# Four banks for a batch's four pieces, and the low-part product as half rows behind them

## The chip, the cores and the metric

The kernel runs on one core of a Trainium2 chip. Its time is the device time of one execution in microseconds, lower is better. Five engines work side by side, each through a queue of its own in order: TensorE (PE, with its weight loads shown apart as PEld), VectorE (DVE), ScalarE (ACT), GpSimd (POOL) and SyncE (SP), which starts the transfers. They wait for each other through semaphores.

## The reference

```python
W = weights[condition]                              # (64, 128, 128)
h = einsum('bct,bcd->bdt', x, W)                    # x: (64, 128, 2048)
logits = einsum('th,eh->te', flat(h), router_weight) + router_bias   # 64 experts, rows of 2048
scores = softmax(logits);  topk_w, topk_idx = top_k(scores, 8)
w_sum = topk_w.sum(-1);    w_dense = scatter of topk_w           # (8192, 64)
out = x + flat(h) * w_sum + w_dense @ expert_bias
```

All data is float32. A row is one of 128 outputs d of one of 64 batches, with 2048 elements t.

## The kernel before

Every matmul that needs float32 accuracy is split: an operand's high part is a copy rounded by ScalarE to the format that TensorE takes in one pass (names in `_hi`), its low part the rest, formed on VectorE or GpSimd (`_lo`), and products of parts are added up in PSUM.

Two batches make a pair (r = 0, 1), and a batch's 2048 columns are four pieces of 512 (n). A pair takes eight slots v. A step i of the pipeline holds three pairs at once: `new` is pair i, whose x is transposed and routed; `mid` is pair i - 1, whose logits, top 8, exponentials and kept weights are worked out; `old` is pair i - 2, which is projected, finished and stored. 32 pairs give 34 steps; 28 steps are a hardware loop of seven turns. The order on each engine is the order written in `step`, nothing reorders it:

- TensorE, slot v: `transposes(i, v)` (four 128x128 into a bank xt_ps; v = 2, 3 are done by VectorE's `relay` instead), `project(i-2, v)` into a bank p_ps, and in some slots `route` (eight matmuls of 256 columns: x transposed times router), `turn_z`, `score`, `turn_kept`.
- ScalarE copies each transposed piece (`xt_high`) and VectorE forms the rest (`xt_low`), which sets the bank free. ScalarE also does `x_high`, `exponentials`, `norm`, `kept_high`.
- VectorE: `xt_low(i, v)`, the top 8 and what follows, `finish(i-2, v)`, which takes a piece out of p_ps, scales it by w_sum, adds x and writes it to out_sb, and `relay`, which writes a transposed piece into a bank of xt_ps from x_turn.
- GpSimd forms x_lo; SyncE loads a batch when the finish eight batches back is done, and stores half a batch once its finishes are done.

PSUM has eight banks: four xt_ps, two p_ps, zt_ps and scores_ps. `project` adds five products per piece: three of x and W, then kept_t_hi and kept_t_lo, each times expert_hl. kept_t (the kept weights over w_sum, transposed) stands twice, in rows 0 to 63 and 64 to 127, and expert_hl holds the experts' high part above and the low part below, so that one product covers both.

Of the kernel before, what the change touches and what calls it, by code (L numbers as in the profile page):

```python
# [40 lines left out]
P = 128  # L41
# [9 lines left out]
def adaln_router(nc, x, condition, weights, router_weight, router_bias, expert_bias, out):  # L51
# [15 lines left out]
    with ExitStack() as ctx:  # L67
# [14 lines left out]
        expert_hl = sb("expert_hl", [P, T], F32R)  # L82

# [32 lines left out]
        xt_ps = [bank(f"xt_ps{i}") for i in range(4)]  # L116
        p_ps = [bank(f"p_ps{i}") for i in range(2)]
# [70 lines left out]
        def steps(eng, step):  # L188
            for j in range(-UNROLL, 0):
                i = UNROLL + j  # L190
                step(0, j, True, i >= 1, i >= 2)
            with eng.Fori(0, LOOPS) as m:
                for j in range(UNROLL):
                    step(m, j, True, True, True)
            step(LOOPS, 0, False, True, True)
            step(LOOPS, 1, False, False, True)
# [15 lines left out]
        def _(sp):  # L212
# [65 lines left out]
            for r in range(2):  # L278
                load(0, 3, r)
                load_weights(0, 3, r)  # L280
                if r == 0:
                    load_turned(0, 3)
                store(0, 0, r)
            with sp.Fori(0, LOOPS) as m:
                for i in range(UNROLL, 2 * UNROLL):
                    for r in range(2):
                        load(m, i, r)
                        load_weights(m, i, r)
                        if r == 0:
                            load_turned(m, i)  # L290
                        store(m, i - 3, r)
# [14 lines left out]
        def _(pe):  # L306
            def transposes(m, o, v):
# [10 lines left out]
                wait(pe, xt_lo_ready, SLOTS * (4 * m + o) + v - 3)  # L318
                for q in range(BLOCKS):
# [5 lines left out]
                    last = pe.transpose(xt_ps[v % 4][:, q * P:(q + 1) * P], block_of_x, ident[:, :])  # L325
# [46 lines left out]

            def project(m, o, v):
# [5 lines left out]
                wait(pe, finished, PIECES * b + n - 1)  # L379
                acc = p_ps[n % 2][:, :]  # L380
# [7 lines left out]
                if v == 0:  # L388
                    pe.wait_ge(kept_t_ready, 4 * m + o + 1)
# [18 lines left out]
            def step(m, j, new, mid, old):  # L408
                i = UNROLL + j
                for v in range(SLOTS):  # L410
                    if new and i == 2 and v < 4:
                        if v == 0:
                            for ahead in range(4):
# [4 lines left out]
                    if mid and v == 7 and i != 1:  # L418
                        turn_kept(m, i - 1)
                    if old:  # L420
                        if i == 2 and v == 0:
                            pe.wait_ge(expert_ready, 1)
# [6 lines left out]
                    if mid and v == 0:  # L429
                        route(m, i - 1, PIECES - 1)  # L430
                    if new and v in ((2, 4, 6) if old else (3, 5, 7)):
# [8 lines left out]
        def _(act):  # L440
            def xt_high(m, o, v):
# [6 lines left out]
                else:  # L448
# [3 lines left out]
                         xt_ps[v % 4][:, :].rearrange("p (q c) -> p q c", c=P)).then_inc(xt_hi_ready, 1)  # L452
# [58 lines left out]
            def step(m, j, new, mid, old):  # L511
                i = UNROLL + j
                for v in range(SLOTS):
# [28 lines left out]
        def _(dve):  # L542
            def xt_low(m, o, v):
                r, n = v % 2, v // 2
                dve.wait_ge(xt_hi_ready, SLOTS * (4 * m + o) + v + 1)
                dve.tensor_tensor(xt_lo[:, n % 2, :, r, :], xt_ps[v % 4][:, :].rearrange("p (q c) -> p q c", c=P),  # L546
                                  xt_hi[:, n % 2, :, r, :].bitcast(F32), ALU.subtract).then_inc(xt_lo_ready, 1)

            def relay(m, o, v):
# [5 lines left out]
                wait(dve, xt_lo_ready, SLOTS * i + v - 3)  # L555
                dve.transpose(xt_ps[v % 4][:, :].rearrange("p (q g c) -> p q g c", g=GROUPS, c=32),  # L556
# [46 lines left out]
            def finish(m, o, v):  # L603
# [8 lines left out]
                dve.scalar_tensor_tensor(out_sb[:, r, cols], p_ps[n % 2][:, :], w_sum[:, o % 2, r:r + 1],  # L612
# [11 lines left out]
            def step(m, j, new, mid, old):  # L624
                i = UNROLL + j
                for v in range(SLOTS):

                    if mid and v == 4:
# [89 lines left out]
```

## Time and profile before

| what | value |
|---|---|
| device time, median of three runs | 559.57 us (558.46 to 559.75) |
| profiled execution, own time | 558.69 us |
| its span | 556.9 us |
| granted TensorE clock, mean | 0.993 |
| busy: PE, DVE, ACT, POOL | 541.0, 471.2, 368.5, 354.4 us |
| DMA | 155.96 MB, 280 GB/s |

The span is the part of the execution that the profile's rows cover. Busy times of PE come from matmuls whose ends are modelled and which overlap, so the distance from one start to the next tells more than a duration.

### The profile page before, as it was taken

How to read it: one execution, taken by the hardware profiler on the slowest of the kernel's cores; microseconds unless marked ns; L12 is line 12 of the kernel's file. 1: busy time of each engine (PE TensorE's matmuls, PEld its weight loads, DVE VectorE, ACT ScalarE, POOL GpSimd, SP SyncE). 2: the span in 40 equal slices, each digit the busy share in tenths (PEclk: the TensorE clock that was granted, in tenths of full speed). 3: DMA queues.
4: the chain of work that ended last, by engine and by line, in shares of the span. 5: the costliest groups of instructions: out<-in, count | busy, mean ns of one | idle time of the engine just before them, and what ended most of it. 6: DMA issues, size and time to landing. Idle time of an engine off the chain costs nothing.

```text
span 556.9 us, 12892 instructions
## 1 busy us (share of the span) xinstructions
PE 541.0 (97%) x3360; PEld 477.0 (86%) x3360; DVE 471.2 (85%) x1055; ACT 368.5 (66%) x836; POOL 354.4 (64%) x326
## 2 busy tenths in 40 slices
PE   5879999999999999999999999999999999999997
PEld 5768888888888888888888888888888888888875
DVE  2488898988889988889988889898888998888975
ACT  3576666677666677666677666667666667766661
POOL 0176666766666776666776666676666677666676
PEclk9979999999999999999999999999999999999999
DMA  8986999888999888898888999888899888889245
GB/s 243 311 201 231 309 297 279 292 300 287 297 318 276 269 311 289 295 325 280 292 276 296 294 311 300 271 290 297 286 298 315 284 283 295 288 294 326 119 166 212
DMA packets 70850, 155.96 MB, mean 280 GB/s; under 512 B 6322, under 2 KB 45234, under 8 KB 62770
## 3 DMA queue, kind: packets, MB, share of 16 engines
q1 hardware_dynamic: 70834, 155.77, 85.6%
q8 instruction: 7, 0.11, 0.1%
q14 instruction: 9, 0.07, 0.0%
HBM read 88.64 MB, written 67.11 MB: 280 GB/s over the span
## 4 chain that ended last, share of the span: by engine, by line
PE 93%; DMA 3%; SPq 1%; ACT 1%; issue 1%; DVE 1%; ACTq 0%; DVEq 0%
PE zt_ps L337 21%; PE xt_ps L325 14%; PE p_ps L390 11%; PE p_ps L387 11%; PE p_ps L385 11%; PE p_ps L386 10%; PE p_ps L391 10%; PE scores_ps L360 2%; DMA out_sb<-L_ffn_expert_bias 2%; PE scores_ps L369 1%; PE scores_ps L351 1%; DMA cond_sb<-itok_B 1%; SPq L243 0%; SPq L244 0%; DVE xt_lo L546 0%
## 5 line engine op out<-in xcount | busy, mean ns | idle before, releaser
L681 POOL TENSOR_TENSOR x_lo<-x_sb,x_hi 128x512 fp32r<-128x512 f32 x256 | 327.0, 1308 | 176.2 <-ACT x_hi L459 176.2
L546 DVE TENSOR_TENSOR xt_lo<-xt_ps,xt_hi 128x512 fp32r<-128x512 f32 x256 | 175.7, 687 | 63.6 <-ACT xt_hi L451 60.8
L451 ACT CAST xt_hi<-xt_ps 128x512 fp32r<-128x512 f32 x256 | 148.2, 582 | 102.9 <-PE xt_ps L325 84.9
L612 DVE SCALAR_TENSOR_TENSOR out_sb<-p_ps,w_sum,x_sb 128x512 f32<-128x512 f32 x256 | 189.6, 740 | 6.2 <-PE p_ps L391 6.2
L459 ACT CAST x_hi<-x_sb 128x1024 fp32r<-128x1024 f32 x128 | 133.7, 1045 | 0.5 <-PE p_ps L391 0.5
L337 PE MATMUL zt_ps<-xt_hi,router_hl 128*128 128x256 f32 x512 | 129.6, 285 | 4.5 <-DVE xt_lo L546 4.5
L337 PE MATMUL zt_ps<-xt_lo,router_hl 128*128 128x256 f32 x512 | 129.2, 285 | 0.0
L325 PE MATMUL xt_ps<-ident,x_sb 128*128 128x128 f32 x784 | 119.2, 277 | 0.1
L385 PE MATMUL p_ps<-x_hi,w_hl 128*128 128x512 f32 x256 | 118.8, 464 | 0.0
L337 PEld LDWEIGHTS zt_ps<-xt_hi,router_hl 128*128 128x128 f32 x512 | 98.1, 192 | 11.0 <-DVE xt_lo L546 5.2
L337 PEld LDWEIGHTS zt_ps<-xt_lo,router_hl 128*128 128x128 f32 x512 | 98.4, 192 | 4.8
L325 PEld LDWEIGHTS xt_ps<-ident,x_sb 128*128 128x128 f32 x784 | 95.0, 145 | 8.5 <-DMA x_sb<-x 0.5
L390 PE MATMUL p_ps<-expert_hl,kept_t_hi 128*128 128x512 f32 x256 | 101.7, 397 | 0.0
L387 PE MATMUL p_ps<-x_hi,w_hl 128*128 128x512 f32 x256 | 101.2, 395 | 0.0
L386 PE MATMUL p_ps<-x_lo,w_hl 128*128 128x512 f32 x256 | 100.5, 393 | 0.0
L391 PE MATMUL p_ps<-expert_hl,kept_t_lo 128*128 128x512 f32 x256 | 100.2, 391 | 0.0
L556 DVE STREAM_TRANSPOSE xt_ps<-x_turn 128x512 f32<-128x512 f32 x60 | 67.2, 1120 | 0.0
L390 PEld LDWEIGHTS p_ps<-expert_hl,kept_t_hi 128*128 128x128 f32 x256 | 48.1, 188 | 11.6 <-DVE kept_t_lo L599 0.8
L391 PEld LDWEIGHTS p_ps<-expert_hl,kept_t_lo 128*128 128x128 f32 x256 | 48.3, 189 | 11.3
L387 PEld LDWEIGHTS p_ps<-x_hi,w_hl 128*128 128x128 f32 x256 | 48.2, 188 | 10.7
L478 ACT ACTIVATE e_all<-logits,neg_max 128x64 f32<-128x64 f32 x64 | 21.8, 340 | 44.1 <-DVE neg_max L579 44.1
L385 PEld LDWEIGHTS p_ps<-x_hi,w_hl 128*128 128x128 f32 x256 | 48.8, 191 | 1.9 <-issue 1.4
(38 smaller groups left out, 368.7 us busy)
## 6 DMA issues: line engine op xcount, KB each, us to landing
out<-out_sb SPq DMA_DIRECT2D x126, 512.0 KB, 4.2
x_sb<-x SPq DMA_DIRECT2D x62, 1024.0 KB, 6.8
x_turn<-x SPq DMA_DIRECT2D x120, 128.0 KB, 4.7
w_sb<-L_cond_weights SPq DMA_DIRECT2D x64, 64.0 KB, 5.3
x_sb<-x SPq DMA_DIRECT2D x4, 256.0 KB, 6.0
x_sb<-x SPq DMA_DIRECT2D x2, 512.0 KB, 8.0
out_sb<-L_ffn_expert_bias SPq DMA_DIRECT2D x2, 512.0 KB, 9.4
out<-out_sb SPq DMA_DIRECT2D x4, 256.0 KB, 2.5
```

Of the source, the lines that this page charges most:

```text
L325: last = pe.transpose(xt_ps[v % 4][:, q * P:(q + 1) * P], block_of_x, ident[:, :])
L337: last = pe.matmul(zt_ps[:, 0:2 * P], router_hl[:, t, :, :].rearrange("p a e -> p (a e)"), xt[:, n % 2, q, :, :].rearrange("p r c -> p (r ...
L385: pe.matmul(acc, w[:, 0, :], x_hi[:, r, cols], start=True, stop=False)
L386: pe.matmul(acc, w[:, 0, :], x_lo[:, r, cols], start=False, stop=False)
L387: pe.matmul(acc, w[:, 1, :], x_hi[:, r, cols], start=False, stop=False)
L390: pe.matmul(acc, kept_t_hi[:, o % 2, r, :], expert_hl[:, cols], start=False, stop=False)
L391: pe.matmul(acc, kept_t_lo[:, o % 2, r, :], expert_hl[:, cols], start=False, stop=True).then_inc(p_ready, 1)
L451: act.copy(xt_hi[:, n % 2, :, r, :], xt_ps[v % 4][:, :].rearrange("p (q c) -> p q c", c=P)).then_inc(xt_hi_ready, 1)
L459: act.copy(x_hi[:, r, cols], x_sb[:, (2 * o + r) % XRING, cols]).then_inc(x_hi_ready, 1)
L546: dve.tensor_tensor(xt_lo[:, n % 2, :, r, :], xt_ps[v % 4][:, :].rearrange("p (q c) -> p q c", c=P), xt_hi[:, n % 2, :, r, :].bitcast(F32) ...
L612: dve.scalar_tensor_tensor(out_sb[:, r, cols], p_ps[n % 2][:, :], w_sum[:, o % 2, r:r + 1], x_sb[:, (2 * o + r) % XRING, cols], ALU.mult, ...
L681: pool.tensor_tensor(x_lo[:, r, cols], x_sb[:, (2 * o + r) % XRING, cols], x_hi[:, r, cols].bitcast(F32), ALU.subtract).then_inc(x_lo_read ...
```

## The change

- **Banks.** xt_ps has two banks in place of four, p_ps four in place of two, one per piece. `transposes` and `relay` of slot v wait for the `xt_low` two slots back, no longer four. `project` of piece n waits for the finish of piece n of the batch before.
- **Products.** `project` leaves out kept_t_lo (but for the last batch). `add_kept_low` does it for all four pieces behind the batch's last projection: kept_t_lo times the experts' high part alone, in half of the rows, pieces 0 and 2 in rows 0 to 63, pieces 1 and 3 in rows 64 to 127. A new tile expert_hh holds the high part in both halves for that. Low part times low part is left out.
- **Finishes.** They come half a pair later: batch 0's four in slots 4 to 7 of its own step, batch 1's in slots 0 to 3 of the next step, each at the start of its slot.
- **Order.** Route 3 moves ahead of projection 0 and route 1 ahead of projection 4. SyncE's stores move by one batch.

```diff
+        expert_hh = sb("expert_hh", [P, T], F32R)
...
-        xt_ps = [bank(f"xt_ps{i}") for i in range(4)]
-        p_ps = [bank(f"p_ps{i}") for i in range(2)]
+        xt_ps = [bank(f"xt_ps{i}") for i in range(2)]
+        p_ps = [bank(f"p_ps{i}") for i in range(PIECES)]
...
                 for i in range(UNROLL, 2 * UNROLL):
-                    for r in range(2):
-                        load(m, i, r)
-                        load_weights(m, i, r)
-                        if r == 0:
-                            load_turned(m, i)
-                        store(m, i - 3, r)
+                    load(m, i, 0)
+                    load_weights(m, i, 0)
+                    load_turned(m, i)
+                    store(m, i - 4, 1)
+                    load(m, i, 1)
+                    load_weights(m, i, 1)
+                    store(m, i - 3, 0)
...
-                wait(pe, xt_lo_ready, SLOTS * (4 * m + o) + v - 3)
+                wait(pe, xt_lo_ready, SLOTS * (4 * m + o) + v - 1)
...
-                wait(pe, finished, PIECES * b + n - 1)
-                acc = p_ps[n % 2][:, :]
+                wait(pe, finished, PIECES * b + n - PIECES + 1)
+                acc = p_ps[n][:, :]
...
-                pe.matmul(acc, kept_t_lo[:, o % 2, r, :], expert_hl[:, cols],
-                          start=False, stop=True).then_inc(p_ready, 1)
+                if is_last(m, o, r):
+                    pe.matmul(acc, kept_t_lo[:, o % 2, r, :], expert_hl[:, cols],
+                              start=False, stop=True).then_inc(p_ready, 1)
+
+            def add_kept_low(m, o, r):
+                pe.wait_ge(kept_t_ready, 4 * m + o + 1)
+                for n in range(PIECES):
+                    rows = slice(n % 2 * E, (n % 2 + 1) * E)
+                    pe.matmul(p_ps[n][:, :], kept_t_lo[rows, o % 2, r, :],
+                              expert_hh[rows, n * PIECE:(n + 1) * PIECE],
+                              start=False, stop=True).then_inc(p_ready, 1)
...
+                    if mid and v == 0:
+                        route(m, i - 1, PIECES - 1)
+                    if new and old and v == 4:
+                        route(m, i, 1)
                     if old:
...
                         project(m, i - 2, v)
                     if mid and v == 3:
                         score(m, i - 1)
+                    if old and v % PIECES == PIECES - 1 and not is_last(m, i - 2, v // PIECES):
+                        add_kept_low(m, i - 2, v // PIECES)
...
-                        act.copy(expert_hl[:, :], expert_sb).then_inc(expert_hi_ready, 1)
+                        act.copy(expert_hh[:, :], expert_sb).then_inc(expert_hi_ready, 1)
+                    if i == 1 and v == 7:
+                        act.copy(expert_hl[0:E, :], expert_sb[0:E, :]).then_inc(expert_hi_ready, 1)
...
-                wait(dve, xt_lo_ready, SLOTS * i + v - 3)
-                dve.transpose(xt_ps[v % 4][:, :].rearrange("p (q g c) -> p q g c", g=GROUPS, c=32),
+                wait(dve, xt_lo_ready, SLOTS * i + v - 1)
+                dve.transpose(xt_ps[v % 2][:, :].rearrange("p (q g c) -> p q g c", g=GROUPS, c=32),
...
+                    if older and v < PIECES:
+                        finish(m, i - 3, PIECES + v)
+                    if old and v >= PIECES:
...
+                        finish(m, i - 2, v - PIECES)
                     if mid and v == 4:
                         dve.wait_ge(logits_ready, 4 * m + i)
                     if new:
...
-                        finish(m, i - 2, v)
```

The first place is TensorE's queue in the loop where batch 0 of a pair ends and batch 1 begins (slots 3 and 4). xt_ps and p_ps carry their bank numbers; ISA and REGISTER_ALU rows set up waits. Before:

```order
L390 MATMUL p_ps1<-expert_hl,kept_t_hi 128x512
L391 MATMUL p_ps1<-expert_hl,kept_t_lo 128x512
L357 ISA
L360 MATMUL scores_ps<-z_sb,w_sb 128x64 x2
L183 REGISTER_ALU
L325 MATMUL xt_ps0<-ident,x_sb 128x128 x4
L378 ISA
L183 REGISTER_ALU
L384 REGISTER_ALU
L385 MATMUL p_ps0<-x_hi,w_hl 128x512
```

Now:

```order
L396 MATMUL p_ps3<-expert_hl,kept_t_hi 128x512
L360 ISA
L363 MATMUL scores_ps<-z_sb,w_sb 128x64 x2
L407 MATMUL p_ps0<-expert_hh,kept_t_lo 128x512
L407 MATMUL p_ps1<-expert_hh,kept_t_lo 128x512
L407 MATMUL p_ps2<-expert_hh,kept_t_lo 128x512
L407 MATMUL p_ps3<-expert_hh,kept_t_lo 128x512
L184 REGISTER_ALU
L328 MATMUL xt_ps0<-ident,x_sb 128x128 x4
L336 REGISTER_ALU
L340 MATMUL zt_ps<-xt_hi,router_hl 128x256
```

The low-part products of all four pieces now stand together between the score and the next batch's transposes, and a route follows the transposes.

The second place is VectorE's queue at the start of a step (slots 0 and 1, and the start of 2 in the second listing). xt_lo rows are `xt_low`, STREAM_TRANSPOSE is `relay`, SCALAR_TENSOR_TENSOR is `finish`. Before:

```order
L546 TENSOR_TENSOR xt_lo<-xt_ps0,xt_hi 128x4x128
L183 REGISTER_ALU
L611 ISA
L612 SCALAR_TENSOR_TENSOR out_sb<-p_ps0,w_sum,x_sb 128x512
L183 REGISTER_ALU
L556 STREAM_TRANSPOSE xt_ps2<-x_turn 128x512
L545 REGISTER_ALU
L546 TENSOR_TENSOR xt_lo<-xt_ps1,xt_hi 128x4x128
L611 REGISTER_ALU
L612 SCALAR_TENSOR_TENSOR out_sb<-p_ps1,w_sum,x_sb 128x512
L556 STREAM_TRANSPOSE xt_ps3<-x_turn 128x512
```

Now:

```order
L636 SCALAR_TENSOR_TENSOR out_sb<-p_ps0,w_sum,x_sb 128x512
L569 ISA
L570 TENSOR_TENSOR xt_lo<-xt_ps0,xt_hi 128x4x128
L580 STREAM_TRANSPOSE xt_ps0<-x_turn 128x512
L635 REGISTER_ALU
L636 SCALAR_TENSOR_TENSOR out_sb<-p_ps1,w_sum,x_sb 128x512
L569 REGISTER_ALU
L570 TENSOR_TENSOR xt_lo<-xt_ps1,xt_hi 128x4x128
L580 STREAM_TRANSPOSE xt_ps1<-x_turn 128x512
L635 REGISTER_ALU
L636 SCALAR_TENSOR_TENSOR out_sb<-p_ps2,w_sum,x_sb 128x512
```

The finish of a slot now stands ahead of the slot's xt_lo and belongs to the batch before; the relay writes the same bank that the xt_lo ahead of it reads.

## Rows read from the trace of the kernel before

**Rows 1.** The chain that ended last, by engine.

```profile
PE 93%; DMA 3%; SPq 1%; ACT 1%; issue 1%; DVE 1%; ACTq 0%; DVEq 0%
```

**Rows 2.** The same chain in time: start us, us, what.

```profile
289.06 0.96 PE zt_ps L337 x8
...
305.59 0.96 PE zt_ps L337 x8
```

**Rows 3.** Stretch: engine busy us (instructions), granted clock, DMA share, GB/s.

```profile
289.06:305.59 16.53, 16.53 (x106) 14.66 (x106) 14.71 (x34) 11.38 (x27) 11.01 (x11) 1.00 0.90 292
```

**Rows 4.** Timeline of TensorE in a pair: start us, us, what.

```profile
291.01 0.55 PE L360 MATMUL scores_ps<-z_sb,w_sb 128*128 128x64 f32 x4
291.40 0.61 PE L325 MATMUL xt_ps<-ident,x_sb 128*128 128x128 f32 x4
291.76 0.47 PE L385 MATMUL p_ps<-x_hi,w_hl 128*128 128x512 f32 x1
292.08 0.39 PE L386 MATMUL p_ps<-x_lo,w_hl 128*128 128x512 f32 x1
...
292.77 0.39 PE L391 MATMUL p_ps<-expert_hl,kept_t_lo 128*128 128x512 f32 x1
293.00 0.28 PE L337 MATMUL zt_ps<-xt_hi,router_hl 128*128 128x256 f32 x1
...
293.96 0.60 PE L325 MATMUL xt_ps<-ident,x_sb 128*128 128x128 f32 x4
...
298.53 0.38 PE L369 MATMUL scores_ps<-ident,kept_twice 128*128 128x128 f32 x2
298.67 0.47 PE L385 MATMUL p_ps<-x_hi,w_hl 128*128 128x512 f32 x1
...
299.91 0.60 PE L325 MATMUL xt_ps<-ident,x_sb 128*128 128x128 f32 x4
```

**Rows 5.** One source line, router transposes: duration ns, first and last start.

```profile
L405 PE MATMUL p_ps<-ident,x_sb x16: 311/311/362, 4.8 to 7.8; 64*128 64x64 f32 x16
```

**Rows 6.** Timeline of TensorE behind the router transposes.

```profile
8.05 1.54 PE L325 MATMUL xt_ps<-ident,x_sb 128*128 128x128 f32 x6
```

**Rows 7.** Timeline of VectorE in a pair.

```profile
288.45 1.12 DVE L556 STREAM_TRANSPOSE xt_ps<-x_turn 128x512 f32<-128x512 f32 x1
289.46 0.68 DVE L546 TENSOR_TENSOR xt_lo<-xt_ps,xt_hi 128x512 fp32r<-128x512 f32 x1
...
295.74 0.69 DVE L546 TENSOR_TENSOR xt_lo<-xt_ps,xt_hi 128x512 fp32r<-128x512 f32 x1 [0.80 <-ACT xt_hi L451]
296.35 0.21 DVE L591 SCALAR_TENSOR_TENSOR e_kept<-e_all,e_rest 128x64 f32<-128x64 f32 x1
...
296.86 0.75 DVE L612 SCALAR_TENSOR_TENSOR out_sb<-p_ps,w_sum,x_sb 128x512 f32<-128x512 f32 x1
...
301.25 0.69 DVE L546 TENSOR_TENSOR xt_lo<-xt_ps,xt_hi 128x512 fp32r<-128x512 f32 x1
301.85 0.74 DVE L612 SCALAR_TENSOR_TENSOR out_sb<-p_ps,w_sum,x_sb 128x512 f32<-128x512 f32 x1
302.51 1.12 DVE L556 STREAM_TRANSPOSE xt_ps<-x_turn 128x512 f32<-128x512 f32 x1
```

**Rows 8.** Timeline of ScalarE in a pair.

```profile
295.15 0.56 ACT L451 CAST xt_hi<-xt_ps 128x512 fp32r<-128x512 f32 x1
...
300.62 0.59 ACT L451 CAST xt_hi<-xt_ps 128x512 fp32r<-128x512 f32 x1 [0.83 <-PE xt_ps L325]
```

**Rows 9.** Group by line: count, busy us, mean ns, idle ahead.

```profile
L520 ACT CAST expert_hl<-out_sb 128x2048 fp32r<-128x2048 f32 x1 | 1.9, 1909 | 2.1 <-DMA out_sb<-L_ffn_expert_bias 2.1
```

**Rows 10.** SyncE's waits: us in total, times, longest.

```profile
SPq L225 <- DVE out_sb L612: 248.5, 98, 8.2
```

**Rows 11.** Two early stretches, columns as in rows 3.

```profile
19.00:25.60 6.60, 5.23 (x41) 4.83 (x42) 3.29 (x6) 3.29 (x8) 0.87 (x2) 1.00 0.97 265
31.30:33.40 2.10, 2.08 (x9) 2.08 (x10) 1.80 (x7) 2.10 (x7) 1.83 (x2) 0.50 1.16 238
```

More of the change, by code:

```diff
@@ L324, in transposes @@
                             "c (k j) -> c j k", k=P)[:, q, :]
-                    last = pe.transpose(xt_ps[v % 4][:, q * P:(q + 1) * P], block_of_x, ident[:, :])
+                    last = pe.transpose(xt_ps[v % 2][:, q * P:(q + 1) * P], block_of_x, ident[:, :])
                 last.then_inc(xt_in_ps, 1)
@@ L371, in turn_kept, with is_last @@
                 last.then_inc(kept_t_in_ps, 1)
+            def is_last(m, o, r):
+                return not is_loop(m) and 8 * m + 2 * o + r == B - 1
             def project(m, o, v):
@@ L406, in _, with step @@
             last.then_inc(router_in_ps, 1)
-            def step(m, j, new, mid, old):
+            def step(m, j, new, mid, old, older):
                 i = UNROLL + j
                 for v in range(SLOTS):
-                    if new and i == 2 and v < 4:
+                    if new and i == 2 and v < 2:
                         if v == 0:
-                            for ahead in range(4):
+                            for ahead in range(2):
                                 transposes(m, i, ahead)
@@ L425, in step @@
                         score(m, i - 1)
+                    if old and v % PIECES == PIECES - 1 and not is_last(m, i - 2, v // PIECES):
+                        add_kept_low(m, i - 2, v // PIECES)
                     if mid and v == 1:
                         turn_z(m, i - 1)
-                    if mid and v == 0:
-                        route(m, i - 1, PIECES - 1)
-                    if new and v in ((2, 4, 6) if old else (3, 5, 7)):
+                    if new and v in ((2, 6) if old else (3, 5, 7)):
                         if i == 0 and v == 3:
@@ L451, in xt_high @@
                 act.copy(xt_hi[:, n % 2, :, r, :],
-                         xt_ps[v % 4][:, :].rearrange("p (q c) -> p q c", c=P)).then_inc(xt_hi_ready, 1)
+                         xt_ps[v % 2][:, :].rearrange("p (q c) -> p q c", c=P)).then_inc(xt_hi_ready, 1)
             def x_high(m, o, r, h):
@@ L509, in _, with step @@
                          p_ps[g][:, :].rearrange("p (t e) -> p t e", e=E)).then_inc(router_hi_ready, 1)
-            def step(m, j, new, mid, old):
+            def step(m, j, new, mid, old, older):
                 i = UNROLL + j
@@ L622, in _, with step @@
                                   ALU.subtract).then_inc(router_ready, 1)
-            def step(m, j, new, mid, old):
+            def step(m, j, new, mid, old, older):
                 i = UNROLL + j
                 for v in range(SLOTS):
+                    if older and v < PIECES:
+                        finish(m, i - 3, PIECES + v)
+                    if old and v >= PIECES:
+                        if i == 2 and v == PIECES:
+                            dve.wait_ge(expert_ready, 1)
+                            dve.wait_ge(expert_hi_ready, 2)
+                        finish(m, i - 2, v - PIECES)
                     if mid and v == 4:
@@ L644, in step @@
                         keep(m, i - 1)
-                    if old:
-                        if i == 2 and v == 0:
-                            dve.wait_ge(expert_ready, 1)
-                        finish(m, i - 2, v)
                     if mid and v == 3:
@@ L682, in x_low, with step @@
                                        x_hi[:, r, cols].bitcast(F32), ALU.subtract).then_inc(x_lo_ready, 1)
-            def step(m, j, new, mid, old):
+            def step(m, j, new, mid, old, older):
                 i = UNROLL + j
```

24 lines of the change are left out of this document (13 added, 11 removed).

## The prediction

> **What bounds the kernel now.** I read the chain of work that ended last first: TensorE holds 93% of it, everything else shares 7% [rows 1]. The same chain, listed in order of time, returns to the same place every 16.53 us (289.06 to 305.59), which is one pair of batches [rows 2]. The table by stretch for that pair shows TensorE busy for all of its 16.53 us at full clock, VectorE for 14.71, ScalarE for 11.38, and the DMA engines at a 0.90 share [rows 3]. So before the change TensorE never waits inside a pair; the reader should see also that VectorE has only 1.8 us a pair to spare.
>
> TensorE's timeline prices its pieces [rows 4]. Four transposes take 0.36 us (291.40 to 291.76). The first matmul of a projection behind transposes takes 0.32 (291.76 to 292.08), a 512-column one otherwise 0.23 (292.77 to 293.00), a route of eight matmuls 0.96 (293.00 to 293.96), the score 0.39 (291.01 to 291.40), and the two transposes of kept_twice 0.14 (298.53 to 298.67). A projection of four matmuls is thus 4 x 0.23 = 0.92, or 1.01 behind transposes or behind a wait. From slot 4's transposes (291.40) to the next pair's slot 0 (299.91) lies 8.51 us, which I call half A; half B is 16.53 - 8.51 = 8.02.
>
> **The change, part by part.** *The products.* For each batch but the last, four full matmuls of kept_t_lo go (4 x 0.23 = 0.92) and four half-row ones come behind its last projection. No row of before shows half-row matmuls side by side. The lower bound is two pairs that run as two matmuls, 0.46. The upper bound is four in a row plus a change of array shape on the way in and out, 0.92 + 2 x 0.25 = 1.42. The 0.25 comes from the one place where 64-row matmuls are followed by 128-row ones: the last router transpose starts at 7.8 [rows 5], the first full one at 8.05 [rows 6]. Between the ends I go by the weight load that each matmul brings: route matmuls with half the columns still stand 0.96 / 8 = 0.12 apart, so I take loads as one per 0.12. Then the last product starts 3 x 0.12 = 0.36 after the first and takes 0.23, 0.59 in all; with 0.08 for each of the two changes of shape (a third of the 0.25, since the start of the kernel runs unlike its middle), 0.75. This alone would gain 2 x (0.92 - 0.75) = 0.34 us a pair.
>
> The Trainium skill ("TensorE: Matmul & The Clock Gate", section "Measured speedup vs the span model") gives packed row tiles the span of one matmul plus about 4 ns a tile; by that the four would take about 0.47 us and the sum below would be 669 in place of the 686 that the rows give. Against the change stands "TensorEngine Tiling (Array Packing)", section "Key Properties": a change of tiling mode drains TensorE. The rows at 7.8 and 8.05 agree with a drain, though they alone don't exclude another cause.
>
> *The wait that the change adds.* This is the large part. With four banks and one per piece, the projection of piece n waits for the finish of piece n of the batch just before, where it waited for the finish two pieces back. All four finishes become possible only when the half-row products are done. VectorE takes its queue in order, and the finishes stand one per slot, each behind the slot before's xt_lo and what follows that. That xt_lo needs the transposes, and they stand on TensorE behind the half-row products, since two transpose banks allow no further lead. TensorE's later pieces (routes, transposes, the score) queue behind the waiting projection. So there is a loop through three engines, and I add it up from the start of the transposes that follow the half-row products to the end of the third finish, which the third projection waits for.
>
> Half A: the order on VectorE here (xt_lo 4, top, finish, xt_lo 5, keep, finish) is unchanged, and before's timeline already holds the path: transposes at 291.40 [rows 4], xt_lo 5 at 295.74, which had waited 0.80 for ScalarE, keep at 296.35, and the finish 296.86 + 0.75 = 297.61 [rows 7]; ScalarE reaches xt_hi 5 only at 295.15 because the exponentials stand ahead of it [rows 8]. That is 297.61 - 291.40 = 6.21 us. It cost nothing before, because TensorE had projections with free banks to do meanwhile.
>
> Half B: transposes at 299.91, xt_hi 0 at 300.62 [rows 8], xt_lo 0 at 301.25 [rows 7]: 1.34. The relay, which turns x_turn into the bank that this xt_lo has just read, must wait for its full end: 0.69 + 0.04. Relay 1.01 (288.45 to 289.46), finish 0.66 (301.85 to 302.51), xt_lo 0.73 as before, relay 1.01, finish to its end 0.75 (all [rows 7]). Sum 1.34 + 0.73 + 1.01 + 0.66 + 0.73 + 1.01 + 0.75 = 6.23.
>
> Behind the third finish TensorE needs 0.05 to start (my estimate, from the 0.04 that other engines take between one's end and the next's start), then in half A a projection 1.01, route 0.96, transposes 0.36, kept_twice 0.14, projection 1.01 and the half-row products 0.75: 6.21 + 0.05 + 3.48 + 0.75 = 10.49, which is 1.98 more than 8.51. In half B: projection 1.01, route 0.96, projection 0.92, score 0.39, products 0.75: 6.23 + 0.05 + 3.28 + 0.75 = 10.31, 2.29 more than 8.02. A pair takes 20.8 us in place of 16.53.
>
> Half A in this form stands in the steps i = 2 to 31, half B in 3 to 31 (in step 2 no older batch is being finished, and the two last steps have no transposes): 30 x 1.98 + 29 x 2.29 = 59.4 + 66.4 = 125.8 us.
>
> *Start and end.* The experts' high part is copied once whole, as before, and then for 64 rows again. The whole copy takes 1.9 us [rows 9], so the second takes 0.95 if it goes with the rows and 1.9 if it goes with the columns; I take 1.9, more work on ScalarE ahead of xt_hi 7 of the second pair and of kept_high, which TensorE waits for there. I count it whole, +2. The end I leave: one batch still uses the old form, and the gain of a batch or two is under 1 us.
>
> *What costs nothing.* The stores move by half a pair, but SP already spent 248.5 us waiting for finishes [rows 10], loads keep their place behind the same finishes, and a slower pair leaves DMA more room than now. Moving route 3 ahead of projection 0 and route 1 ahead of projection 4 only reorders TensorE's work; it covers the first finish of a batch (0.36 + 0.96 behind the products, against some 0.4 + 0.75), not the second and third.
>
> The sum: 558.69 (the profiled execution; the median of three is 559.57, 0.2% above) + 125.8 + 2 = 686 us.
>
> **The rivals.**
> *Serial products.* The change would not do what it says if the half-row products don't overlap: with 1.42 in place of 0.75 each half is 0.67 longer, 59 x 0.67 = 40, so 726. Nothing in the rows of before excludes it. 12%.
>
> *Only one half waits.* If VectorE's path were some 2 us shorter in one half (the exponentials earlier in A, the relays shorter in B), about 620 to 627. The 6.21 of half A is read off one stretch, which speaks against it there; half B is put together. 8%.
>
> *The clock falls.* TensorE would be idle 4.6 us of each 20.8 (20.8 - 16.53 + 0.34), in pieces of about 1.2. Between 19.00 and 25.60 it was busy 5.23 of 6.60, the same share, and the granted clock stayed 1.00, its 2.4 GHz level; between 31.30 and 33.40, after an idle stretch of several us, it was 0.50, the 1.2 GHz level [rows 11]. If a tenth of the some 16 us of TensorE work in a pair fell to the lower level, 1.6 x 29.5 = 47 more: about 735 and up. 5%.
>
> *Faster.* If the finishes came in time, TensorE would stay the bound and the pair would shrink by 0.34 (0.92 at best): 558.7 - 30 x 0.34 = 548, down to 531. It decides from the point where the third finish ends 4.0 us after the transposes (transposes 0.36, route 1.05 behind them, projection 0.92, transposes 0.36, projection 1.01, transposes 0.36 in half A; 3.8 in half B, where two transposes of 0.14 stand in place of the last) where I have 6.2. Only VectorE at a much lighter load could do that; 4%.
>
> **How the numbers follow.** My forecast (both halves wait, products near 0.75) holds 71%, by itself from 669 (products at 0.46, 59 x 0.29 = 17 less) to 705. With the serial case the range from 658 to 728 leaves out the one-sided wait, the low clock and the faster case, and so about two in ten. About 0.3% is what a measurement of this kernel can tell from no change. Slower: 71 + 12 + 8 + 5 = 96, of which I move one to "same" for mixtures: slower 0.95, same 0.01, faster 0.04.
>
> **What would show it.** In the profile after: waits of TensorE on VectorE's finish of about 4 to 5 us a pair, at the projections of the second and third piece; ScalarE's wait for transposes grown; a pair of 20 to 21.5 us; VectorE's busy time per pair unchanged at about 14.7, its share down to about 70%. The half-row matmuls: a start-to-start of 0.12 or less within a pair confirms the overlap, 0.23 the serial rival. The prediction is wrong if TensorE still fills the chain with no such waits, or if the finish of piece 3, not 2, is what is waited for.

## The result and the profile after

The changed kernel takes 712.66 us (median of four runs, 712.31 to 713.14) where the kernel before takes 559.66 in the same comparison: a ratio of 1.2734, with a 95% interval of 1.2705 to 1.2763. The forecast was 686 us, slower, with a range of 658 to 728.

First the chain that ended last in the changed kernel, by engine. It answers to [rows 1], where TensorE alone held 93%.

```profile
PE 45%; DVE 20%; issue 16%; ACT 13%; DMA 3%; POOL 1%; SPq 1%; ACTq 1%; DVEq 1%; POOLq 0%
```

The chain now goes round TensorE, ScalarE and VectorE. The waits of the changed kernel say where (engine, line, what it waited for: us in total, times, longest us):

```profile
ACT xt_hi L473 <- PE xt_ps L328: 252.4, 124, 6.4
DVE xt_lo L570 <- ACT xt_hi L473: 143.6, 130, 4.9
PEld p_ps L391 <- DVE out_sb L636: 130.5, 112, 1.5
PE p_ps L391 <- DVE out_sb L636: 109.6, 120, 1.3
```

TensorE's first matmul of a projection (L391) waits 120 times for a finish (L636), ScalarE for transposes, VectorE for ScalarE: each engine of the loop waits for the one ahead of it. TensorE's timeline in one pair shows which projections wait (start us, us, what, idle before; it answers to [rows 4]):

```profile
327.28 0.73 PE L407 MATMUL p_ps<-expert_hh,kept_t_lo 64*128 64x512 f32 x4
327.94 0.66 PE L328 MATMUL xt_ps<-ident,x_sb 128*128 128x128 f32 x4
...
330.31 0.60 PE L328 MATMUL xt_ps<-ident,x_sb 128*128 128x128 f32 x4
331.57 0.50 PE L391 MATMUL p_ps<-x_hi,w_hl 128*128 128x512 f32 x1 [0.66 <-DVE out_sb L636]
...
332.61 0.60 PE L328 MATMUL xt_ps<-ident,x_sb 128*128 128x128 f32 x4
334.21 0.50 PE L391 MATMUL p_ps<-x_hi,w_hl 128*128 128x512 f32 x1 [1.00 <-DVE out_sb L636]
...
337.57 0.40 PE L396 MATMUL p_ps<-expert_hl,kept_t_hi 128*128 128x512 f32 x1
337.89 0.73 PE L407 MATMUL p_ps<-expert_hh,kept_t_lo 64*128 64x512 f32 x4
338.56 0.65 PE L328 MATMUL xt_ps<-ident,x_sb 128*128 128x128 f32 x4
...
340.93 0.60 PE L328 MATMUL xt_ps<-ident,x_sb 128*128 128x128 f32 x4
342.55 0.50 PE L391 MATMUL p_ps<-x_hi,w_hl 128*128 128x512 f32 x1 [1.02 <-DVE out_sb L636]
...
343.58 0.38 PE L354 MATMUL scores_ps<-ident,zt_sb 128*128 128x128 f32 x2
344.93 0.50 PE L391 MATMUL p_ps<-x_hi,w_hl 128*128 128x512 f32 x1 [0.97 <-DVE out_sb L636]
```

These are the second and third piece of each half, 3.65 us of waiting a pair. The waits are counted from modelled ends, here 0.60 us behind the start of four transposes that otherwise take 0.36. From start to start, with 0.36 for four transposes and 0.14 for two, the same four places lose 0.90, 1.24, 1.26 and 1.21: 4.61 us a pair. VectorE's timeline in both halves gives the finish that the third piece waits for; it answers to [rows 7]:

```profile
332.33 0.69 DVE L570 TENSOR_TENSOR xt_lo<-xt_ps,xt_hi 128x512 fp32r<-128x512 f32 x1 [0.81 <-ACT xt_hi L473]
...
333.43 0.72 DVE L636 SCALAR_TENSOR_TENSOR out_sb<-p_ps,w_sum,x_sb 128x512 f32<-128x512 f32 x1
...
344.18 0.70 DVE L636 SCALAR_TENSOR_TENSOR out_sb<-p_ps,w_sum,x_sb 128x512 f32<-128x512 f32 x1
```

The first of these finishes ends at 334.15, and the projection starts at 334.21; the second ends at 344.88, and the projection starts at 344.93. The transposes of kept_twice mark the pairs. In the changed kernel they stand in steps 2 and 31 at:

```profile
56.63 0.38 PE L372 MATMUL scores_ps<-ident,kept_twice 128*128 128x128 f32 x2
...
681.23 0.38 PE L372 MATMUL scores_ps<-ident,kept_twice 128*128 128x128 f32 x2
```

and in the kernel before:

```profile
50.53 0.38 PE L369 MATMUL scores_ps<-ident,kept_twice 128*128 128x128 f32 x2
...
530.00 0.38 PE L369 MATMUL scores_ps<-ident,kept_twice 128*128 128x128 f32 x2
```

Between them lie 29 pairs: 624.60 / 29 = 21.54 us each, where before had 479.47 / 29 = 16.53. Of the 154.4 us that the span grew (711.3 against 556.9), the 29 pairs hold 145.1, the start 6.1 and the end 3.2. Both chains wait for the experts' transfer at the start. Here are the row of the kernel before, that of the changed kernel, and a row from the end of the changed kernel's chain (start us, us, what):

```profile
14.71 10.41 DMA out_sb<-L_ffn_expert_bias
...
14.26 14.00 DMA out_sb<-L_ffn_expert_bias
...
693.37 6.26 POOL x_lo L708 x5
```

The pair at 325 us, whose rows stand above, takes 21.04, not 21.54. The rest is the clock. The windows of 1 us in another pair (busy us of PE, PEld, DVE, ACT, POOL, then granted clock, DMA share, GB/s) show it:

```profile
298.00:299.00 1.00, 0.05 (x1) 0.05 (x1) 1.00 (x3) 1.00 (x3) 1.00 (x2) 1.00 1.20 259
...
300.00:301.00 1.00, 0.36 (x3) 0.12 (x1) 1.00 (x2) 0.69 (x3) 0.93 (x1) 1.00 1.00 387
301.00:302.00 1.00, 0.67 (x2) 0.57 (x3) 1.00 (x3) 0.28 (x1) 1.00 (x2) 0.78 0.28 111
302.00:303.00 1.00, 1.00 (x3) 0.75 (x3) 1.00 (x3) 0.00 (x0) 1.00 (x3) 0.50 0.00 0
...
304.00:305.00 1.00, 1.00 (x6) 1.00 (x6) 0.00 (x0) 0.00 (x0) 0.00 (x0) 0.52 1.03 397
305.00:306.00 1.00, 1.00 (x7) 0.83 (x7) 0.00 (x0) 0.00 (x0) 0.00 (x0) 1.00 0.92 209
```

Behind half B's two gaps (298 and 300) the granted clock stands at 0.50, the 1.2 GHz level, for some 3.4 us. A route then takes 1.71 us in the chain in place of 0.96 [rows 2], and the four matmuls ahead of it 0.43 each in place of 0.23: some 1.6 us for one such dip. Nine routes of the chain are lengthened (to between 1.45 and 1.71 us), most of them some 64.6 us apart, which is every third pair. The pairs between have the same gaps: behind 342.55 and 344.93 above nothing is lengthened. 9 x 1.6 = 14.4, and 29 x 4.51 (21.04 - 16.53) = 130.8: together the 145.1.

### The profile page after: what moved, and what is told of

Same layout as the page of the kernel before. It is cut to its first block, busy times and chain, and to the rows that moved or that the text cites. A ratio compares the mean times of both kernels' runs of the same rounds, so it can differ in the third digit from the quotient of the medians.

```text
span 711.3 us, 12965 instructions
## 1 busy us (share of the span) xinstructions
PE 578.3 (81%) x3360; PEld 459.4 (65%) x3360; DVE 479.4 (67%) x1055; ACT 371.8 (52%) x837; POOL 352.9 (50%) x326
## 4 chain that ended last, share of the span: by engine, by line
PE 45%; DVE 20%; issue 16%; ACT 13%; DMA 3%; POOL 1%; SPq 1%; ACTq 1%; DVEq 1%; POOLq 0%
PE zt_ps L340 9%; DVE out_sb L636 9%; ACT xt_hi L473 7%; PE xt_ps L328 7%; PE p_ps L391 7%; DVE xt_lo L570 6%; PE p_ps L407 6%; PE p_ps L392 4%; PE p_ps L396 4%; PE p_ps L393 4%; ACT e_all L500 2%; ACT e_rest L504 2%; DMA out_sb<-L_ffn_expert_bias 2%; PE scores_ps L363 2%; DVE e_kept L615 2%
## 5 line engine op out<-in xcount | busy, mean ns | idle before, releaser
L391 PE MATMUL p_ps<-x_hi,w_hl 128*128 128x512 f32 x256 | 118.6, 463 | 112.8 <-DVE out_sb L636 109.6
L636 DVE SCALAR_TENSOR_TENSOR out_sb<-p_ps,w_sum,x_sb 128x512 f32<-128x512 f32 x256 | 187.5, 736 | 7.2 <-PE p_ps L407 4.1
L391 PEld LDWEIGHTS p_ps<-x_hi,w_hl 128*128 128x128 f32 x256 | 49.3, 193 | 143.5 <-DVE out_sb L636 130.5
L340 PE MATMUL zt_ps<-xt_hi,router_hl 128*128 128x256 f32 x512 | 139.8, 303 | 0.0
L340 PE MATMUL zt_ps<-xt_lo,router_hl 128*128 128x256 f32 x512 | 133.9, 292 | 0.0
L328 PE MATMUL xt_ps<-ident,x_sb 128*128 128x128 f32 x784 | 123.8, 282 | 10.0 <-DVE xt_lo L570 9.8
L340 PEld LDWEIGHTS zt_ps<-xt_hi,router_hl 128*128 128x128 f32 x512 | 102.6, 200 | 3.7 <-DVE xt_lo L570 0.6
L340 PEld LDWEIGHTS zt_ps<-xt_lo,router_hl 128*128 128x128 f32 x512 | 102.8, 201 | 3.1
L392 PE MATMUL p_ps<-x_lo,w_hl 128*128 128x512 f32 x256 | 103.3, 403 | 0.0
L392 PEld LDWEIGHTS p_ps<-x_lo,w_hl 128*128 128x128 f32 x256 | 50.0, 195 | 0.3
L594 DVE TENSOR_TENSOR logits<-scores_ps,bias_sb 128x128 f32<-128x128 f32 x32 | 9.3, 291 | 58.1 <-PE scores_ps L363 58.1
L407 PE MATMUL p_ps<-expert_hh,kept_t_lo 64*128 64x512 f32 x252 | 46.2, 444 | 0.0
```

The source lines that it names most:

```text
L328: last = pe.transpose(xt_ps[v % 2][:, q * P:(q + 1) * P], block_of_x, ident[:, :])
L340: last = pe.matmul(zt_ps[:, 0:2 * P], router_hl[:, t, :, :].rearrange("p a e -> p (a e)"), xt[:, n % 2, q, :, :].rearrange("p r c -> p (r ...
L391: pe.matmul(acc, w[:, 0, :], x_hi[:, r, cols], start=True, stop=False)
L392: pe.matmul(acc, w[:, 0, :], x_lo[:, r, cols], start=False, stop=False)
L407: pe.matmul(p_ps[n][:, :], kept_t_lo[rows, o % 2, r, :], expert_hh[rows, n * PIECE:(n + 1) * PIECE], start=False, stop=True).then_inc(p_re ...
L636: dve.scalar_tensor_tensor(out_sb[:, r, cols], p_ps[n][:, :], w_sum[:, o % 2, r:r + 1], x_sb[:, (2 * o + r) % XRING, cols], ALU.mult, ALU. ...
```

## The experiments

Expected pairs and times are against the changed kernel unless the text says otherwise. Ratios are to the kernel before.

**Full rows.** The low-part products keep their place but run over all rows, as before the change.

```diff
-                    pe.matmul(p_ps[n][:, :], kept_t_lo[rows, o % 2, r, :],
-                              expert_hh[rows, n * PIECE:(n + 1) * PIECE],
+                    pe.matmul(p_ps[n][:, :], kept_t_lo[:, o % 2, r, :],
+                              expert_hl[:, n * PIECE:(n + 1) * PIECE],
```

> The changed kernel, but the four low-part products behind a batch's last projection take all 128 rows (kept_t_lo times expert_hl, low times low included) in place of half rows; nothing else differs. If the half-row products run side by side (four within 0.66 us, 0.75 with the way in), full ones take 4 x 0.23 = 0.92 and stand in the loop of waits twice a pair: 2 x 0.17 x 30 = about 10 us slower than the changed kernel, 723. If half rows gain nothing, the time stays at 713; if their change of array shape costs more than they save, it falls to 705 or less.

Measured: 713.2 us (711.96 to 718.54), ratio 1.2777 (1.2718 to 1.2836), which cannot be told from the changed kernel. But the clock differs between the two: 0.988 here against 0.974, with only four dips in the loop, the last at 218 us. An undisturbed pair takes 21.32 us, 0.28 more. So the time did not settle what the half rows are worth; the next run but one (early finishes, full rows) does, without dips. Behind the last dip the clock stays up for 483 us, although half B's two gaps stand in every pair as they did (TensorE's timeline, then the stretch, columns as above):

```profile
409.29 0.50 PE L391 MATMUL p_ps<-x_hi,w_hl 128*128 128x512 f32 x1 [1.02 <-DVE out_sb L635]
...
411.68 0.50 PE L391 MATMUL p_ps<-x_hi,w_hl 128*128 128x512 f32 x1 [0.96 <-DVE out_sb L635]
```

```profile
222.00:705.00 483.00, 401.89 (x2341) 332.29 (x2340) 335.08 (x748) 254.86 (x581) 250.16 (x226) 1.00 0.66 218
```

**Early finishes.** The same products and banks, but two finishes each in the first two slots of a half, and a few small steps moved out of their way.

```diff
-                    if older and v < PIECES:
-                        finish(m, i - 3, PIECES + v)
+                    if older and v < PIECES:
+                        for n in ((0, 1), (2, 3), (), ())[v]:
+                            finish(m, i - 3, PIECES + n)
...
-                        finish(m, i - 2, v - PIECES)
+                        for n in ((0, 1), (2, 3), (), ())[v - PIECES]:
+                            finish(m, i - 2, n)
```

> The changed kernel, but VectorE's finishes stand earlier in its queue: pieces 0 and 1 at the start of a batch's first slot, 2 and 3 at the start of the second (z_sum goes ahead of xt_lo 2, and ScalarE's second x_high behind kept_high). Banks, products and TensorE's order stay. Theory (the third finish is late because of what stands ahead of it on VectorE): TensorE's waits for finishes nearly vanish, a pair falls from 21.5 to some 16.7 us, 29 x 4.8 = 140 us less, 560 to 585 in all, and the clock stays at its upper level. Rival 1 (two transpose banks set the pace) and rival 2 (the half-row products and their change of array shape do): stays above 690.

Measured: 576.38 us (575.07 to 577.31), ratio 1.0294 (1.0263 to 1.0326). TensorE's waits for finishes are gone in this kernel, and a wait of its weight loads for xt_lo has come:

```profile
PE p_ps L391 <- DVE out_sb L636: 0.2, 1, 0.2
```

```profile
PEld zt_ps L340 <- DVE xt_lo L570: 23.8, 60, 0.5
```

The pair is 16.94 us on the mean. Nine tenths of the loss (136 of 153 us, the dips of the clock included) go with the place of the finishes in VectorE's queue; banks, products and stores are the same. The few steps that moved along were not moved alone in any run.

**Early finishes with full rows.** Both edits together.

> Both halves' finishes in pairs of slots as in e2_early_finish, and the low products over full rows as in e1_full_rows, so that the clock dips do not hide what the half rows are worth. If a group of four full-row products takes 0.92 to 1.01 us where the half rows take 0.66 to 0.76, the pair is 0.3 to 0.5 longer than e2's 16.94: 576.4 + 29 x 0.4 = 588 us (584 to 592). If the half rows are worth nothing on the path, 576 us.

Measured: 583.71 us (582.75 to 583.81), ratio 1.0425 (1.0407 to 1.0443). Neighbouring pairs in this kernel:

```profile
311.80 0.38 PE L372 MATMUL scores_ps<-ident,kept_twice 128*128 128x128 f32 x2
...
329.01 0.38 PE L372 MATMUL scores_ps<-ident,kept_twice 128*128 128x128 f32 x2
```

The pair of 17.21 is 0.27 above 16.94, just below what was expected, and 29 x 0.27 = 7.8 answers to the 7.3 us in the times. So the half rows are worth 0.27 us a pair, 0.13 a group; the 0.28 of the undisturbed pairs of full rows agrees.

**One half alone.** Half A's finishes early (first run), or half B's (second run), by the same edit in one of its two places.

> The changed kernel, but only half A (batch 1's projections) gets the early finishes: on VectorE the finishes of pieces 0 and 1 stand ahead of xt_lo 4, those of 2 and 3 ahead of xt_lo 5, and ScalarE's second x_high stands behind kept_high. Theory (each half has a loop of its own, of about 2 us a pair): half A falls to some 8.5 us, half B keeps some 10.4, so about 650 us, half of the way to the 576 of the kernel with both. Rival (one shared cause, so that either remedy alone is enough or neither helps alone): near 576 or near 713.

> The changed kernel, but only half B (batch 0's projections) gets the early finishes: the older batch's finishes of pieces 0 and 1 ahead of xt_lo 0, those of 2 and 3 ahead of xt_lo 1, z_sum ahead of xt_lo 2. Theory as for half A: half B falls to some 8.4 us, half A keeps some 10.6, about 645 us. Rival: near 576 or near 713.

Half B early: 640.3 us (one run), pair 19.02, as expected. Half A early: 674.29 us (one run), 24 us above what was expected, although half A itself took the 8.5 us that I had put (328.47 to 337.01, from transposes to transposes). TensorE's timeline in this kernel shows where the rest went, in half B:

```profile
320.52 0.50 PE L391 MATMUL p_ps<-x_hi,w_hl 128*128 128x512 f32 x1 [1.02 <-DVE out_sb L636]
...
322.91 0.80 PE L391 MATMUL p_ps<-x_hi,w_hl 128*128 128x512 f32 x1 [0.98 <-DVE out_sb L636]
323.51 0.63 PE L392 MATMUL p_ps<-x_lo,w_hl 128*128 128x512 f32 x1
```

Behind the second gap a matmul of 512 columns takes 0.63 in place of 0.39 (granted clock 0.50 from 323 to 326), and this in 26 of the 29 pairs, all but the first three: 20.34 on the mean, mean clock 0.928. So one half less to wait gave less than it should because the clock fell more often. That was an inference until the next run but one.

**Filled gaps.** In the changed kernel TensorE gets spare products of 256 columns in three of the four places where it waited, into columns of a bank that nobody reads. They bring no finish forward.

```diff
+FILL = {2: 7, 5: 5, 6: 8}
...
+                    if older and new and v in FILL:
+                        for _ in range(FILL[v]):
+                            pe.matmul(zt_ps[:, 2 * P:4 * P], router_hl[:, 0, :, :].rearrange("p a e -> p (a e)"),
+                                      expert_hh[:, 0:2 * P], start=v == 2, stop=v == 2)
```

> The changed kernel with matmuls of 256 columns added on TensorE just ahead of the waits for finishes, in three of the four gaps of a pair: 7 ahead of piece 2 in half B, 5 and 8 ahead of pieces 1 and 2 in half A. They write columns of zt_ps that nobody reads, so the output is unchanged. They take 0.12 us each and fit into gaps of 0.7 to 1.0 us, so by the theory the loop and the pair of 21.04 us stay as they are. If the nine stretches at the lower clock level come from TensorE's gaps, they go, and with them 14 us: about 699. If they have another cause, 713. If the loop is not what sets the pace and TensorE's work is, 20 x 0.12 x 29 = 70 us more.

Measured: 699.86 us (699.43 to 700.89), ratio 1.2504 (1.2481 to 1.2527), with 580 more matmuls than the changed kernel. No dip is left in the loop, and the pair is 21.08. More work took 13 us less.

**Half A early, half B's gap filled.** The same fill, in slot 2 alone, in the kernel with half A early.

> e5_early_a with seven products of 256 columns added in each step, on a bank that is written again before it is read, ahead of the second half's products for the third piece, where TensorE stood for about 1.0 us. They fill a gap and shorten no wait: the finishes stand where they stood in e5. Clock theory: the 40 us that e5 missed are the lower clock behind the second half's gaps; with one of the two gaps filled the clock stays up, the pair is 8.54 + 10.42 = 18.96 instead of 20.34, and the time is 674 - 29 x 1.38 = 634 us (628 to 642), granted clock over 0.98. Rival: e5's first half gave its 2 us back to a longer second half by the order of the work; then the fill changes nothing or costs, 674 us or more.

Measured: 637.07 us (one run), clock 0.994. Rows of one pair:

```profile
301.23 0.38 PE L372 MATMUL scores_ps<-ident,kept_twice 128*128 128x128 f32 x2
...
307.13 0.50 PE L391 MATMUL p_ps<-x_hi,w_hl 128*128 128x512 f32 x1 [1.02 <-DVE out_sb L640]
308.30 1.07 PE L443 MATMUL zt_ps<-expert_hh,router_hl 128*128 128x256 f32 x7
309.52 0.50 PE L391 MATMUL p_ps<-x_hi,w_hl 128*128 128x512 f32 x1 [0.15 <-DVE out_sb L640]
...
320.20 0.38 PE L372 MATMUL scores_ps<-ident,kept_twice 128*128 128x128 f32 x2
```

The pair is 18.97, expected 18.96. With one gap of the two filled (0.15 left of it) the clock stays up, and the time is 37 us below that of the early half A alone.

**A smaller relay.** VectorE's two relays a pair move a quarter of the columns.

```diff
-                dve.transpose(xt_ps[v % 2][:, :]....,
-                              x_turn[:, o % 2, r, :, :]....)
+                dve.transpose(xt_ps[v % 2][:, 0:P]....,
+                              x_turn[:, o % 2, r, :, :]....[:, 0:1])
```

> The changed kernel, but each relay turns only a quarter of its piece (128 of 512 columns; the rest of the bank keeps old values, so the second piece's routing is left out in three quarters). Theory: the loop of waits of half B holds two relays of 1.04 us; at some 0.3 each, half B is 1.5 us shorter and half A as long as before, so a pair of about 19.6 and about 670 us in all. Rival (the banks alone, or the products, or the clock set the pace): within 10 us of 713.

Measured: 670.52 us (one run), pair 20.13, where 19.6 was expected; the time matches because the clock stayed higher (0.995) than I had counted with, which is luck. Each relay became 0.7 us shorter, but the second xt_lo of half B now waits 0.39 us for ScalarE's copy, which the theory had left out. So the relays are on half B's path, as its sum had them, for 0.9 us of the 1.4 that they lost.

**Two transpose banks alone.** The kernel before with two banks of xt_ps, nothing else.

```diff
-        xt_ps = [bank(f"xt_ps{i}") for i in range(4)]
+        xt_ps = [bank(f"xt_ps{i}") for i in range(2)]
...
-                wait(pe, xt_lo_ready, SLOTS * (4 * m + o) + v - 3)
+                wait(pe, xt_lo_ready, SLOTS * (4 * m + o) + v - 1)
```

> The kernel before, with two transpose banks in place of four and nothing else changed (p_ps keeps two). Theory: in the timeline of before each transposition starts at least 0.2 us after the xt_lo two slots back has ended, so inside a pair nothing waits, and only the start loses some us: 560 to 566 us. Rival (fewer transpose banks are what made the changed kernel slow): above 600 us.

Measured: 561.94 us (560.66 to 564.96), ratio 1.0043 (1.0021 to 1.0064), with pairs of 16.53. The shorter lead alone costs 2 us, and none of it in the pairs. What it adds once the finishes are late no run shows, since no kernel has late finishes and four transpose banks.

**Regrouped.** The changed kernel's parts in another order on all three engines, with the early finishes and transposes of two slots together. T are transposes, R routes, P projections, AL low-part products, TZ, S, TK the turn of z, the score, the turn of kept. First TensorE's order in the first run, then in the second:

```diff
-T0 T1 R3 P0 P1 P2 R0 P3 TZ AL0 T4 T5 S R1 P4 P5 P6 P7 T6 TK T7 AL1 R2
+T0 T1 R3 P0 P1 P2 R0 P3 TZ AL0 T4 T5 S R1 P4 P5 P6 P7 T6 T7 TK AL1 R2
```

> The changed kernel's banks and products with another order on three engines: TensorE issues transposes in twos and three projections in a row, and the last route of a pair behind the half-row products; VectorE does a batch's finishes first; ScalarE's exponentials stand behind xt_hi 5. Theory: with the finishes early and fewer places where a matmul follows transposes (0.09 us each), a pair can fall below the 16.53 of the kernel before, to 15.8 to 16.3 us: 540 to 556, faster than before by 1 to 3%. If the two transpose banks or ScalarE's chain bind in this order, 17 us a pair or more, 575 and up.

> e8_regrouped with one exchange in TensorE's order: the transposes of slot 7 ahead of those of kept, so that kept's copies have some 0.6 us more. The wait of kept's transposes for the copy, 9.3 + 0.6 us over 32 times or 0.3 us a pair, should go: 568.2 - 29 x 0.3 = 559.5 us (555 to 564), about the time of the kernel before. Rival: the copies of slot 7, which stand behind kept's on ScalarE, pass the wait on to the next step's first transposes; then 568 us or a little more.

Measured: 568.2 us (565.29 to 570.12), ratio 1.0161 (1.0136 to 1.0186), a miss: the pair was 16.59. Then, with T7 ahead of TK, 561.14 us (558.95 to 564.86), ratio 1.0034 (1.0014 to 1.0054), inside what was expected. Its pair:

```profile
316.22 0.38 PE L372 MATMUL scores_ps<-ident,kept_twice 128*128 128x128 f32 x2
...
332.62 0.38 PE L372 MATMUL scores_ps<-ident,kept_twice 128*128 128x128 f32 x2
```

16.40 us: 0.13 less than before, 3.9 us over the loop. The products' share of it and that of the new order were not separated, since this order was not run with full rows. But the first of these rows in the loop stands at 53.83 and the last at 529.37, in a span of 559.2: 3.3 us more than before at the start and 2.9 at the end, which is more than the loop gives.

**Another order at the ends.** The second regrouped kernel, with the copy of the experts' low rows behind that of slot 7 at the start, and in the step that follows the last transposes this order on TensorE (and the like on the others):

```diff
+R3 P0 P1 TZ P2 S P3 AL0 P4 P5 P6 P7 AL1 TK
```

> e11_regrouped_two with another order in the first and the last steps alone; the loop's order stays. e11's pair takes 16.40 us against 16.53 before, so its loop is 29 x 0.13 = 3.9 us shorter than that of the kernel before, and its span is 2.3 longer, so that 6.2 us lie ahead of and behind the loop. At the start the copy of the experts' low part (1.80 us on ScalarE, on the chain) goes behind the copy of slot 7, for which TensorE stood 2.2 us: 1.8 less. At the end the router's last transposes, scores and exponentials go ahead of products and finishes, and the low products ahead of kept's transposes, so that the cast of the last batch's x starts before 544.4 and GpSimd's last four pieces end before 550.6: 1.5 to 5 less. Sum 561.1 - 1.8 - 3 = 556 us (553 to 558), below the kernel before. Rival: what the first copy waits for comes no sooner, and GpSimd, with 14 pieces of 1.25 us at the end, sets the end in any order: 559 to 561.

Measured: 562.22 us (561.6 to 565.04), ratio 1.0058 (1.0037 to 1.0079): a miss. The chain of this kernel at the start, a stretch near the end (columns as above), and GpSimd's last pieces:

```profile
34.26 2.29 DVE expert_hl L746
```

```profile
547.20:550.40 3.20, 3.20 (x9) 2.55 (x8) 1.50 (x3) 0.29 (x1) 3.20 (x4) 0.50 0.68 274
```

```profile
546.63 5.00 POOL L787 TENSOR_TENSOR x_lo<-x_sb,x_hi 128x512 fp32r<-128x512 f32 x4 [2.30 <-ACT x_hi L512]
```

At the start VectorE's own part of expert_hl, 2.29 us, took the place of ScalarE's copy; at the end GpSimd's last four pieces came 1.1 us later than without the edit (545.52), since the order of the finishes held up the last projection and with it the products that the cast waits for. In the profiled run TensorE also did the batch ahead of the last at the lower clock, behind a wait of 1.68 us, with 0.43 in place of 0.23 us for a matmul of 512 columns. No version beat the kernel before.

## Why the prediction was right, and what it missed

**The mechanism** was the one forecast, step by step, and in both halves. Half A's path from the transposes to the third finish, read off the timeline of before as 6.21 us, is 327.94 to 334.15: 6.21. Half B's, put together from single rows as 6.23, is 338.56 to 344.88 by VectorE's timeline: 6.32. The halves take 10.62 and 10.42 (forecast 10.49 and 10.31). The waits stand at the second and third piece, as written; the sign of 4 to 5 us a pair is missed by the waits in the profile (3.65) and met from start to start (4.61, as the forecast had it). The early finishes show the cause by experiment: with them the loop opens and 136 us are gone; each half alone gives its own part (half B measured 2.0 us a pair, half A 2.1 once the gap was filled).

**The range** was met with luck. The forecast by itself went from 669 to 705, and 712.66 lies above that. It is inside the range only because the range was drawn out to 728 for products in series, and that is not what happened.

**The products** were put at 0.75 us a group. In the pair above they take 0.66 (327.28 to 327.94) and, with the step ahead, 338.56 - 337.80 = 0.76, where 337.80 is 337.57 plus 0.23. The serial rival (1.42) is refuted. But the make-up of the 0.75 was wrong, and that its sum came out is luck. TensorE's timeline, taken in two short windows, shows the group as two and two:

```profile
327.28 0.50 PE L407 MATMUL p_ps<-expert_hh,kept_t_lo 64*128 64x512 f32 x2
...
327.62 0.39 PE L407 MATMUL p_ps<-expert_hh,kept_t_lo 64*128 64x512 f32 x2
```

Two products on different halves of the rows start 3 ns apart, where the sum had 0.12 us. The second two start 0.34 us behind the first two, and the transposes 0.32 behind those, where full-row products stand 0.23 apart [rows 4]. So two products do run as one matmul, as the lower bound said, but as a slower one; why it takes 0.33 us no run shows. The Trainium skill ("TensorE: Matmul & The Clock Gate", section "Measured speedup vs the span model") puts packed tiles about 4 ns apart. For two that run together the trace agrees, with 3 ns; where the prediction's estimate from that page gave 0.47 us for the group, 0.66 was measured.

**What was mis-sized.** The sum was 127.8 us, the span grew by 154.4. The missing 26.6 split as follows:
- 7.0 in the pair itself, 29 x 0.24: half A was 0.13 longer and half B 0.11, in half B nearly all on VectorE's path (0.09). In half A 0.08 of it is the four transposes ahead of kept_twice, 336.21 to 336.65, for which the sum took 0.36; the kernel before has them at 0.43 too (298.10 to 298.53).
- 14.3 in the clock. I held the low clock to be a rival of its own with 5%, at no less than 47 us, because an early stretch with the same busy share had kept 1.00 [rows 11]. It came as a term of the likeliest case instead, nine short dips. What misled was to judge by the mean busy share: the one long gap of that early stretch (1.34 us, up to 23.37) stands alone, while each dip came behind half B's two gaps of 1 us close together. By its gain of 13 us the filled kernel shows that without the gaps there are no dips in the loop; the full rows show that the gaps alone don't bring one each time. The gap in the kernel before:

```profile
23.37 0.63 PE L360 MATMUL scores_ps<-z_sb,w_sb 128*128 128x64 f32 x4 [1.34 <-POOL w_hl L671]
```

- 2.1 at the start: 6.1 against the 2 for the second copy plus one half A (1.98). The rows take the 6.1 apart otherwise. The experts' transfer landed 3.1 us later (28.26 in place of 25.12), and no run shows that this comes from the change. From there to the first transposes of kept_twice (34.90 before, 40.62 now) 2.6 came, of which the second copy is 1.80, near the 2 of the forecast. From there to the next such transposes only 0.4 came, although half A's wait is in it: before, the first products of that stretch had run at the lower clock, and now they did not.
- 3.2 at the end, which I had put at nothing. There two late finishes (686.78 and 689.79) stand on the chain, behind them exponentials and an x_hi, and then GpSimd's casts from 693.37 to 702.13; the last batch's projection starts only at 702.74. In the kernel before no cast of GpSimd is on the chain at the end. The regrouped kernel has casts on its chain too, and kept 2.9 there without waits for finishes in the loop.

**The faster rival** needed the third finish by 4.0 us behind the transposes. With the finishes moved forward by hand the waits went, but the pair still was no shorter than before (16.94), and routes waited for xt_lo instead; only a new order of three engines brought 16.40, and the ends took that back.

## What to carry to other kernels

A product that is moved behind a group makes every consumer of the group late at once; before counting the matmuls it saves, follow the freed banks round through the queues of the other engines, and add up the loop from one point back to the same point. Where an engine takes its queue in order, the place of the consumer in the queue can matter more than the number of banks: here it was worth 136 us, the products 8, and the two transpose banks by themselves 2. A forecast in which TensorE starts to idle in short gaps needs a term for its clock.

## What the runs showed of the hardware

- Every dip of the clock in the loop stood behind half B's two gaps of about 1 us close together, but these gaps did not bring one in every pair. In the changed kernel the clock fell in 9 of 29 pairs, for some 3.4 us; in the kernel with only half B's gaps it fell in 26; with full rows in four, and then not for 483 us; with one of the two gaps filled by spare matmuls, in none. With only half A's gaps (0.67 and 1.01 us) it never fell in the loop either. What decides from pair to pair is not shown. The Trainium skill ("TensorE: Matmul & The Clock Gate", section "A second HAM failure mode: psum-queue depth-cycling") tells of a kernel that goes round its PSUM banks and idles shortly between groups of matmuls, often enough for the clock to swing between its levels; these runs agree, 699.86 against 712.66 us.
- So TensorE can gain by useless work: 580 matmuls more, 13 us less.
- Two products on different halves of the rows start together (3 ns apart), but the next two only 0.34 us later. Four of them in place of four full ones were worth 0.13 us, not half of 0.92.
- The mean clock is not the same in each run of one program: four runs of the full rows stood at 0.974 to 0.988, and the one at 0.974 took 718.54 us, the others 711.96 to 713.25. A difference of 8 us in such a kernel is told apart only once the gaps are gone.
